# A four-layer graph kernel: two biases given by one-row products, two row weightings on VectorE

## The chip, the core and the metric

The kernel runs on one core of a Trainium2 chip. Five engines work side by side, each through its own queue in order: TensorE (PE), VectorE (DVE), ScalarE (ACT), GpSimd (POOL) and SyncE (SP, which only issues DMAs). They wait for each other by semaphores. The metric is the device time of one execution in microseconds (us), as the median of several.

## What is computed

50,000 nodes with 256 features each, 25,000 edges (12,500 pairs, both ways) and a loop at every node pass through four graph layers, each with a residual and a normalisation. Cut to what matters:

```python
x = layernorm(x + L0(x))          # two hypergraph convolutions, PReLU
# L1: attention over edges, 8 heads of 32
sent = x @ W_s + b_s;  recv = x @ W_r + b_r
logits = einsum(leaky_relu(sent[src] + recv[dst]), a_w) + a_b
w = softmax of logits over the edges of each dst
x = layernorm(x + segment_sum(w * sent[src], dst))
# L2: attention, 4 heads of 32, then a projection
x = layernorm(x + (segment_sum(alpha * h[src], dst) + bias) @ Wp + bp)
# L3: attention, 4 heads of 64, relu, rows divided by their norm
x = layernorm(x + L3(x))
```

The weights of one node sum to one, so `b_s` goes through the sum of L1 unchanged. In L2 the two biases come out as one row, called `bc`.

## The kernel before, in words

Nodes are split in two kinds. Those with edges are sorted into 50 groups of 512 rows (`ng` = 50, four chunks `k` of 128), and pass through seven stages, `p` = 0 to 6, group by group; `q = p * 50 + i` names a group in a stage. Stages 0 to 2 are the hops of L0. Stage 3 ends L0 and prepares L1 (its time in the profile is about 1820 to 2810 us). Stage 4 is L1's attention and the preparation of L2 (to 3890 us), stage 5 is L2's attention and projection (to 4610 us), stage 6 is L3 (to the end, 5534 us). A stage begins when the last has stored its tables. The nodes without edges need only dense products: the **dense pipeline**, 49 blocks of 512 rows (`dense_parts`), which may run at any time from stage 1 on.

The order on each engine isn't written by hand. `schedule` lists every step with its engine (T TensorE, S ScalarE, V VectorE, G GpSimd, Y SyncE), name and group, what it comes after, and its length from the table `TOOK`; the planner `Plan.run` lays the steps out, and each engine's queue follows that order. So a longer entry in `TOOK` also moves the dense blocks, which fill the gaps.

Steps that the change touches, by their names:

- Stage 3, per group: `x1b` (VectorE, L2113 and four row additions L2053 in `add_rows`) makes the rows of L1's input; `norm` (ScalarE, L1463) normalises them into `res`; `tp0`, `tp1` turn them (L1061) into `xl_t`. `tab0`, `tab1` multiply by `ws` (L1070) to give `sent`, and `r0`, `r1` multiply by `wr`, with `br` added in L2129 for `recv`. `ez` (L2138, L2141) forms the leaky sum in `z`, or in `sm` for some groups. `ew` on GpSimd (L2535) multiplies it by the attention weights `aw`. `es` on VectorE (L2145, L2147) sums to logits. `br` holds `b_r` plus `b_s`, since `tab` has no bias.
- `xb` on GpSimd (L2547), stages 3 and 4: after the rows have been turned, it adds the bias row to `res` (`bs_c` in stage 3 for L1, `bc` in stage 4 for L2), and `xst` (SyncE, L2736) stores the sum as the residual that the next stage loads into `xo`.
- Stage 4: `vals` (VectorE, L2286, L2287) weights the gathered rows; `mine` on GpSimd (L2541, L2542) weights the group's own rows by `pp`. `agg0` to `agg3` on TensorE (L1273) sum the chunks, and VectorE carries a row from one chunk to the next (L2161, L2163) and adds the own rows (L2315). `merge` divides (L2333) and adds the residual (L2053).
- Stage 5: `wp0`, `wp1` multiply by `wp` (L1283), and VectorE adds `xo` (L2343).
- Stage 4 has besides, on VectorE, the leaky sum of the edges' logits (L2188) and a running maximum (L2235), and on TensorE small products (L1261, L1262). The dense pipeline's lines are L1910 to L1969 and the statistics after them on VectorE, and L1061, L1070, L1083, L1107 and L1114 on TensorE.
- GpSimd also issues all gathers and scattered stores (L2460, L2456, L2551) and takes small powers (L2518, 128x4).

## Time and profile before

| | us |
|---|---|
| median of 3 runs | 5526.51 |
| lowest, highest | 5526.36, 5539.13 |
| the profiled execution, its own time | 5536.22 |
| its span | 5534.1 |
| TensorE clock granted, mean | 0.833 |
| device memory moved | 919.07 MB, 166 GB/s |

All durations below come from the one profiled execution, whose own time is 10 us above the median; 2 us of it lie outside the span. A busy time counts a moment once, however many instructions overlap in it, while a mean or median is of single instructions. An instruction that an engine has begun and that stands still counts as busy.

### The profile page before, as it was taken

The numbers are of one execution on the slowest core, as the hardware profiler recorded it, in microseconds if no ns is written. First come the engines' busy times: TensorE is split into PE (matmuls) and PEld (weight loads), VectorE is DVE, ScalarE is ACT, GpSimd is POOL, SyncE is SP. The second block draws the span as 40 slices with busy tenths as digits, with TensorE's granted clock in tenths as the row PEclk, the third lists the DMA queues.
The fourth block names the chain that finished last, engine by engine and source line by source line (L and its number), as shares of the span: only waits on it lengthen the run. The fifth ranks groups of instructions, "written<-read, shape, count | busy, mean of one in ns | idle before, by whom it ended". The sixth has DMA issues, their size and how long they took to land. (4 is left out here: it accounts for less than half of the span.)

```text
span 5534.1 us, 80216 instructions
## 1 busy us (share of the span) xinstructions
PE 4378.5 (79%) x19786; PEld 3284.9 (59%) x19786; DVE 3950.4 (71%) x10982; ACT 3033.9 (55%) x8955; POOL 3477.4 (63%) x2992
## 2 busy tenths in 40 slices
PE   0674349999999988888888898888899998767664
PEld 0541126666776767767666676666777786555442
DVE  8732114445776789888878777788888887888886
ACT  0233235555898666665654454455544556666655
POOL 2777777764777766666556556565644435777786
PEclk9855569999999999989998888888898999776555
DMA  1887644444666555555344444443455553444453
GB/s 41 274 288 267 189 131 149 153 161 140 222 217 205 189 179 176 191 174 180 143 141 156 143 158 160 147 157 125 121 181 182 195 185 124 133 136 125 147 156 99
DMA packets 360952, 919.07 MB, mean 166 GB/s; under 512 B 70931, under 2 KB 144781, under 8 KB 360496
## 3 DMA queue, kind: packets, MB, share of 16 engines
q1 hardware_dynamic: 250048, 639.69, 34.2%
q0 software_dynamic: 110448, 274.25, 16.5%
q8 instruction: 170, 2.79, 0.2%
q14 instruction: 286, 2.34, 0.1%
HBM read 578.85 MB, written 340.23 MB: 166 GB/s over the span
## 5 line engine op out<-in xcount | busy, mean ns | idle before, releaser
L2460 POOL DMA_INDIRECT got<-tab,end_i x600 | 700.7, 1168 | 481.7 <-PE psum L1273 319.6
L1158 PE MATMUL psum<-got,sf 128*128 128x256 f32 x1600 | 622.6, 477 | 353.4 <-ACT got L1425 279.4
L2460 POOL DMA_INDIRECT got<-hop,end_i x600 | 631.1, 1052 | 285.5 <-issue 166.7
L1158 PEld LDWEIGHTS psum<-got,sf 128*128 128x128 f32 x1600 | 327.2, 227 | 570.8 <-DMA got<-in_x,src_i 218.5
L1273 PE MATMUL psum<-got,sf 128*128 128x264 f32 (+2 forms) x1200 | 449.0, 463 | 266.6 <-DVE got L2164 166.8
L1425 ACT COPY got<-psum 1x256 f32<-1x256 f32 x796 | 282.3, 355 | 387.8 <-PE psum L1158 318.4
L1273 PEld LDWEIGHTS psum<-got,sf 128*128 128x128 f32 x1200 | 232.6, 231 | 391.2 <-DVE got L2164 222.6
L2090 DVE TENSOR_TENSOR res<-psum,own 128x512 f32<-128x512 f32 x300 | 206.4, 688 | 338.4 <-DMA own<-in_x,node_i 149.7
L1463 ACT ACTIVATE res<-res,l_mo 128x256 f32<-128x256 f32 x600 | 309.9, 588 | 185.2 <-DVE l_mo L2044 184.7
L1315 ACT ACTIVATE squares<-res,l_sv 128x256 f32<-128x256 f32 x600 | 296.9, 497 | 168.0 <-DVE l_sv L2056 110.4
L1429 ACT ACTIVATE res<-res,invc 128x256 f32<-128x256 f32 x600 | 270.8, 498 | 210.3 <-DVE res L2090 209.5
L1411 ACT CAST sf<-s 128x512 f32<-128x512 uint8 x350 | 214.4, 613 | 283.7 <-DVE s L2071 150.2
L2460 POOL DMA_INDIRECT x_in<-in_x,dn_i x196 | 219.1, 1118 | 145.4 <-PE psum L1061 67.6
L2518 POOL TENSOR_TENSOR l_mo<-l_mo,power 128x4 f32<-128x4 f32 x150 | 170.9, 1140 | 204.3 <-DVE l_mo L2121 202.3
L2551 POOL DMA_INDIRECT out<-res,out_i x200 | 235.1, 1175 | 98.8 <-issue 57.2
L1061 PE MATMUL psum<-ident,res 128*128 128x128 f32 x1600 | 257.2, 286 | 32.7 <-ACT res L1429 16.3
L2456 POOL DMA_INDIRECT out<-hd,dn_i x196 | 222.8, 1137 | 91.1 <-issue 53.6
L1303 ACT COPY xl_t<-psum 128x512 f32<-128x512 f32 x400 | 230.8, 580 | 82.0 <-PE psum L1061 79.4
L1061 PEld LDWEIGHTS psum<-ident,res 128*128 128x128 f32 x1600 | 202.2, 148 | 94.7 <-issue 38.2
L2460 POOL DMA_INDIRECT own<-in_x,node_i x200 | 208.9, 1045 | 72.9 <-issue 57.5
L2053 DVE SCALAR_TENSOR_TENSOR res<-res,xo 128x256 f32<-128x256 f32 x400 | 244.1, 664 | 3.4
L2460 POOL DMA_INDIRECT got<-in_x,src_i x200 | 204.2, 1021 | 60.9 <-issue 58.8
(497 smaller groups left out, 13253.6 us busy)
## 6 DMA issues: line engine op xcount, KB each, us to landing
own<-hop SPq DMA_DIRECT2D x150, 512.0 KB
x_t<-res SPq DMA_DIRECT2D x150, 512.0 KB, 2.7
xo<-x_t SPq DMA_DIRECT2D x150, 512.0 KB
hop<-res SPq DMA_DIRECT2D x100, 512.0 KB, 4.5
tab<-tab SPq DMA_DIRECT2D x50, 536.0 KB
own<-tab SPq DMA_DIRECT2D x50, 536.0 KB
r_t<-rec_b SPq DMA_DIRECT2D x50, 528.0 KB, 2.9
rec_b<-r_t SPq DMA_DIRECT2D x50, 528.0 KB, 3.9
```

What stands on the lines that cost most here:

```text
L1061: i = T.transpose(o[:, k * P:(k + 1) * P], src[:, k, c * P:(c + 1) * P], ident[:])
L1158: T.matmul(o, sf_of(q)[:, k * P:(k + 1) * P], got_of(q)[:, k * FEAT:(k + 1) * FEAT], start=(p < 3), stop=True).then_inc(at("l_agg"), 1)
L1273: T.matmul(bank(3 + k % 2)[:, 0:g.ext], sf_[:, k * P:(k + 1) * P], got_of(q)[:, k * g.width:k * g.width + g.ext], start=True, stop=True).t ...
L1303: S.copy(dst, filled_bank(eng, name, q)[:, 0:dst.shape[1]]).then_inc(at("s_out"), 1)
L1315: i = S.activation(squares[:, k, :], src[:, k, :], ACT.Square, bias=bias, scale=scale, accum_out=acc[:, k:k + 1])
L1425: S.copy(got_of(to)[0:1, c * FEAT:(c + 1) * FEAT], bank(3 + h // 2)[0:1, (h % 2) * FEAT:(h % 2 + 1) * FEAT]).then_inc(at("l_carry"), 1)
L1429: m = S.mul(res_of(q)[:, k, :], res_of(q)[:, k, :], invc[:, k, i:i + 1])
L1463: m = S.activation(res_of(q)[:, k, :], res_of(q)[:, k, :], ACT.Identity, bias=l_mo[:, par, 7, k:k + 1], scale=l_mo[:, par, 6, k:k + 1])
L2053: m = V.scalar_tensor_tensor(res_of(q)[:, k, :], res_of(q)[:, k, :], 0.0, xo_of(q)[:, k, :], ALU.add, ALU.add, accum_out=l_sv[:, par, 0, k ...
L2456: eng.indirect_dma_start(out=out, out_offset=bass.IndirectOffsetOnAxis(ap=dn_i[:, d * K + k:d * K + k + 1], axis=0), in_=hd[:, d % 3, k, : ...
L2460: eng.indirect_dma_start(out=dst, out_offset=None, in_=table, in_offset=bass.IndirectOffsetOnAxis(ap=idx, axis=0), bounds_check=rows_ - 1, ...
L2551: eng.indirect_dma_start(out=out, out_offset=bass.IndirectOffsetOnAxis(ap=out_i[:, k, i:i + 1], axis=0), in_=res_of(q)[:, k, :], in_offset ...
```

## The change

Four things change. `xb` is gone from GpSimd: `res` is stored as it is. In its place the bias enters the product: `tab0` and `tab1` of stage 3 (`biased_product`) and `wp0` and `wp1` of stage 5 begin each of their two sums with a product of a row of ones and the bias row, over one row of contraction. `br` loses `bs_c`, since `tab` now carries it. The multiplication by `aw` goes from GpSimd into `es` on VectorE, and stage 4's `mine` goes to VectorE. Additions into `res` wait for `l_sh` besides. `TOOK` and the steps' lengths follow.

```diff
-    "Tscan": 0.44, "Tspr": {4: 1.75, 5: 0.88, 6: 0.88}, "Tt3t": 0.44, "Ttab0": {3: 1.73, 4: 0.93, 5: 0.91}, "Ttab1": {3: 1.73, 4: 0.93, 5: 0.91},
+    "Tscan": 0.44, "Tspr": {4: 1.75, 5: 0.88, 6: 0.88}, "Tt3t": 0.44, "Ttab0": {3: 2.59, 4: 0.93, 5: 0.91}, "Ttab1": {3: 2.59, 4: 0.93, 5: 0.91},
-    "Ves": 1.56, "Vez": 2.77, "Vfrs": 0.22, "Vh": 0.66, "Vhd": 0.79, "Vlead": {4: 0.92, 5: 0.2, 6: 0.34}, "Vlogit": 0.66,
-    "Vmax": {4: 0.55, 5: 0.15, 6: 0.15}, "Vmerge": {4: 4.16, 5: 1.15, 6: 1.68}, "Vmine": {5: 0.62, 6: 1.15}, "Vmo": 0.83, "Vnode": 0.15, "Voh": 0.42,
+    "Ves": 2.76, "Vez": 2.77, "Vfrs": 0.22, "Vh": 0.66, "Vhd": 0.79, "Vlead": {4: 0.92, 5: 0.2, 6: 0.34}, "Vlogit": 0.66,
+    "Vmax": {4: 0.55, 5: 0.15, 6: 0.15}, "Vmerge": {4: 4.16, 5: 1.15, 6: 1.68}, "Vmine": {4: 1.4, 5: 0.62, 6: 1.15}, "Vmo": 0.83, "Vnode": 0.15, "Voh": 0.42,
...
-                    put(("V", "x1b", q), 2.95, here("Sx1a") + ([("S", "sqv", q - 2)] if i >= 2 else []))
+                    put(("V", "x1b", q), 2.95, here("Sx1a") + ([("S", "sqv", q - 2), ("V", "sh", q - 2)] if i >= 2 else []))
-                if p < 5:
-                    put(("G", "xb", q), 2.5, here("Ttp0", "Ttp1"))
-                put(("Y", "xst", q), 0.35, here("Snorm" if p == 5 else "Gxb"), landing=3.0)
+                put(("Y", "xst", q), 0.35, here("Snorm"), landing=3.0)
-                put(("G", "ew", q), 2.8, here("Vez"))
-                put(("V", "es", q), 1.6, here("Gew"))
+                put(("V", "es", q), 2.8, here("Vez"))
-                me = "Gmine" if p == HOPS else "Vmine"
-                put((me[0], "mine", q), 3.1 if p == HOPS else 0.75, here("Sexp", "Yown"))
+                put(("V", "mine", q), 1.4 if p == HOPS else 0.75, here("Sexp", "Yown"))
-                    put(("V", f"agg{k}", q), 0.78 if p != 5 else 0.5, here(f"Tagg{k}", me))
+                    put(("V", f"agg{k}", q), 0.78 if p != 5 else 0.5, here(f"Tagg{k}", "Vmine"))
-                put(("V", "merge", q), {4: 3.2, 5: 1.0, 6: 1.7}[p], here("Vagg3") + ([("S", "sqv", q - 2)] if p == 4 else []) + free_ + (here("Yxo") if p == 4 else []) + early("V", "merge", 1))
+                put(("V", "merge", q), {4: 3.2, 5: 1.0, 6: 1.7}[p], here("Vagg3") + ([("S", "sqv", q - 2), ("V", "sh", q - 2)] if p == 4 else []) + free_ + (here("Yxo") if p == 4 else []) + early("V", "merge", 1))
-                put(("V", "u", q), 1.8, here("Grn", "Yxo") + [("S", "sqv", q - 2)] * (i >= 2))
+                put(("V", "u", q), 1.8, here("Grn", "Yxo") + [("S", "sqv", q - 2), ("V", "sh", q - 2)] * (i >= 2))
...
+        def biased_product(eng, name, q, h, rows_t, w, bias):
+
+            o = free_bank(eng, name, q)
+            for k in (2 * h, 2 * h + 1):
+                here = o[:, (k % 2) * FEAT:(k % 2 + 1) * FEAT]
+                T.matmul(here, ones[:], bias[0:1, :], start=True, stop=False)
+                for c in range(2):
+                    if k == 2 * h:
+                        eng.wait_ge(at("s_out"), ev_no[f"tp{c}", q])
+                    i = T.matmul(here, rows_t[:, c, k * P:(k + 1) * P], w[:, c, :], start=False, stop=(c == 1))
+            i.then_inc(at("t_fill"), 1)
...
+                rows_t = xl_t[:, large["xl"].slot(q)]
+                if p == 3:
+                    biased_product(eng, name, q, h, rows_t, ws, bs_c)
+                    return
                 for c in range(2):
                     eng.wait_ge(at("s_out"), ev_no[f"tp{c}", q])
-                rows_t = xl_t[:, large["xl"].slot(q)]
-                if p == 3:
-                    half_product(eng, name, q, h, rows_t, ws)
-                elif p == 4:
+                if p == 4:
...
-                eng.wait_ge(at("s_out"), ev_no["tz", q])
                 o = free_bank(eng, name, q)
                 for k in (2 * h, 2 * h + 1):
                     here = o[:, (k % 2) * FEAT:(k % 2 + 1) * FEAT]
-                    m = T.matmul(here, zt[:, k * P:(k + 1) * P], wp[:], start=True, stop=True)
+                    T.matmul(here, ones[:], bc[0:1, :], start=True, stop=False)
+                    if k == 2 * h:
+                        eng.wait_ge(at("s_out"), ev_no["tz", q])
+                    m = T.matmul(here, zt[:, k * P:(k + 1) * P], wp[:], start=False, stop=True)
...
+                V.memset(ones[:], 1.0)
...
+                done(V.tensor_tensor(br[:], br[:], bs_c[:], ALU.subtract))
...
             if ln_of(q) >= 2:
                 eng.wait_ge(at("d_sq"), sq_done["sqv", q - 2][1])
                 eng.wait_ge(at("l_nm"), ln_of(q) - 1)
+                eng.wait_ge(at("l_sh"), ln_of(q) - 1)
...
             elif name == "es":
                 rows_ = by_chunk(rec_of(q), recv_w)
+                zh = z_of(q).rearrange("p (m c) -> p m c", c=cols1)
+                eng.wait_ge(at("l_ez"), i + 1)
+                V.tensor_tensor(zh, zh, over(aw[:], K * heads1), ALU.mult).then_inc(at("l_ew"), 1)
                 eng.wait_ge(at("l_ew"), i + 1)
...
+            elif name == "mine" and p == HOPS:
+                eng.wait_ge(at("g_p"), j + 1)
+                eng.wait_ge(*own_landed(q))
+                c4, weight = split_heads(own_f, g), by(pp[:, par, 1, 0:hk])
+                V.tensor_tensor(c4, c4, weight.unsqueeze(3).to_broadcast([P, K, g.heads, g.cols]), ALU.mult)
+                V.tensor_copy(own_f[:, :, g.flat:g.ext], weight).then_inc(at("g_w"), 1)
...
-            elif name == "ew":
-                eng.wait_ge(at("l_ez"), i + 1)
-                zh = z_of(q).rearrange("p (m c) -> p m c", c=cols1)
-                G.tensor_tensor(zh, zh, over(aw[:], K * heads1), ALU.mult).then_inc(at("l_ew"), 1)
-            elif name == "mine":
-                eng.wait_ge(at("g_p"), i + 1)
-                eng.wait_ge(*own_landed(q))
-                own_f = by_chunk(own_of(q), g1.width)
-                c4, weight = split_heads(own_f, g1), pp[:, par, 1, 0:K * heads1].rearrange("p (k h) -> p k h", k=K)
-                G.tensor_tensor(c4, c4, weight.unsqueeze(3).to_broadcast([P, K, heads1, cols1]), ALU.mult)
-                G.tensor_copy(own_f[:, :, g1.flat:g1.ext], weight).then_inc(at("g_w"), 1)
-            elif name == "xb":
-
-                eng.wait_ge(at("l_ln"), ln_of(q) + 1)
-                eng.wait_ge(at("t_fill"), max(fill_no["tp0", q], fill_no["tp1", q]) + 1)
-                G.tensor_tensor(res_of(q), res_of(q), over((bs_c if p == 3 else bc)[:], K), ALU.add).then_inc(at("l_xb"), 1)
...
-                    eng.wait_ge(at("l_xb"), q - stop_a + 1)
+                    eng.wait_ge(at("l_ln"), ln_of(q) + 1)
```

The planner then gives other orders. GpSimd, from the first groups of stage 3 on, before:

```order
L2547 TENSOR_TENSOR res<-res,bs_c 128x1024
L2518 TENSOR_TENSOR l_mo<-l_mo,power 128x4
L2460 DMA got<-hop,end_i 128x256 x4
L2460 DMA x_in<-in_x,dn_i 128x256 x4
L2535 TENSOR_TENSOR z<-z,aw 128x1024
L2547 TENSOR_TENSOR res<-res,bs_c 128x1024
L2460 DMA got<-hop,end_i 128x256 x4
L2535 TENSOR_TENSOR z<-z,aw 128x1024
L2518 TENSOR_TENSOR l_mo<-l_mo,power 128x4
```

and now:

```order
L2485 DMA got<-hop,end_i 128x256 x4
L2485 DMA x_in<-in_x,dn_i 128x256 x4
L2543 TENSOR_TENSOR l_mo<-l_mo,power 128x4
L2485 DMA got<-hop,end_i 128x256 x4
L2481 DMA out<-hd,dn_i 50000x256 x4
L2543 TENSOR_TENSOR l_mo<-l_mo,power 128x4
```

The 128x1024 operations on rows are gone; gathers, stores and the 128x4 powers remain.

VectorE, where a group of stage 3 ends (`z` the leaky sum, `rec_b` the receiver rows), before:

```order
L2138 TENSOR_TENSOR z<-tab,rec_b 128x1024
L2141 SCALAR_TENSOR_TENSOR z<-z 128x1024
L1931 BN_STATS d_bn<-psum 128x6 x2
L2129 TENSOR_TENSOR rec_b<-psum,br 128x2x256
L2145 TENSOR_REDUCE rec_b<-z 128x4x8
L2147 SCALAR_TENSOR_TENSOR rec_b<-rec_b,ab,hostc 128x4x8
L2129 TENSOR_TENSOR rec_b<-psum,br 128x2x256
L2113 SCALAR_TENSOR_TENSOR res<-z,oma,res 128x1024
```

and now:

```order
L2153 TENSOR_TENSOR z<-tab,rec_b 128x1024
L2156 SCALAR_TENSOR_TENSOR z<-z 128x1024
L2123 SCALAR_TENSOR_TENSOR res<-psum,invc,xo 128x256 x2
L2161 TENSOR_TENSOR z<-z,aw 128x1024
L2163 TENSOR_REDUCE rec_b<-z 128x4x8
L2165 SCALAR_TENSOR_TENSOR rec_b<-rec_b,ab,hostc 128x4x8
L1945 BN_STATS d_bn<-psum 128x6 x2
L2144 TENSOR_TENSOR rec_b<-psum,br 128x2x256
L2128 SCALAR_TENSOR_TENSOR res<-z,oma,res 128x1024
```

The product with `aw` (L2161) stands between the leaky sum and the reduction, with one other group's step ahead of it.

TensorE in the middle of stage 5 (`t3w` the next layer's weights, `got` the gathered rows), before:

```order
L1238 MATMUL psum<-ms,sm 128x8 x4
L1076 MATMUL psum<-t3w,xl_t 128x268 x2
L1283 MATMUL psum<-wp,lgt 128x256 x2
L1076 MATMUL psum<-t3w,xl_t 128x268 x2
L1283 MATMUL psum<-wp,lgt 128x256 x2
L1076 MATMUL psum<-t3w,xl_t 128x268 x2
L1273 MATMUL psum<-got,sf 128x132
L1076 MATMUL psum<-t3w,xl_t 128x268 x2
```

and now:

```order
L1283 MATMUL psum<-got,sf 128x132
L1085 MATMUL psum<-t3w,xl_t 128x268 x2
L1292 MATMUL psum<-bc,ones 128x256
L1295 MATMUL psum<-wp,lgt 128x256
L1292 MATMUL psum<-bc,ones 128x256
L1295 MATMUL psum<-wp,lgt 128x256
L1283 MATMUL psum<-got,sf 128x132
L1260 MATMUL psum<-ident,fmax 128x4 x4
```

Each product with `wp` has a product with `bc` in front.

The dense blocks move too. Counted in the two orders on TensorE, the first product of 20, 33, 41 and 44 of the 49 blocks stood ahead of the first product of stages 3, 4, 5 and 6; now it is 20, 30, 37 and 40. Stage 3 thus holds 10 instead of 13 blocks, stage 4 holds 7 instead of 8, stage 5 holds 3 as before, and stage 6 holds 9 instead of 5. On GpSimd the stores of dense rows (`out<-hd`) now stand among the very last entries:

```order
L2560 DMA out<-res,out_i 50000x256 x4
L2481 DMA out<-hd,dn_i 50000x256 x4
L2551 TENSOR_TENSOR l_ss<-l_ss,power 128x4 x2
L2543 TENSOR_TENSOR l_mo<-l_mo,power 128x4 x2
L2560 DMA out<-res,out_i 50000x256 x4
L2551 TENSOR_TENSOR l_ss<-l_ss,power 128x4
L2560 DMA out<-res,out_i 50000x256 x4
L2481 DMA out<-hd,dn_i 50000x256 x4
L2543 TENSOR_TENSOR l_mo<-l_mo,power 128x4
L2481 DMA out<-hd,dn_i 50000x256 x4
L2560 DMA out<-res,out_i 50000x256 x4
```

Before, the last of them stood 65 rows ahead of the end.

## Rows read from the trace of the kernel before

**Rows 1.** busy time, share of the span, instructions of each engine: part 1 of the page
```profile
PE 4378.5 (79%) x19786; PEld 3284.9 (59%) x19786; DVE 3950.4 (71%) x10982; ACT 3033.9 (55%) x8955; POOL 3477.4 (63%) x2992
```

**Rows 2.** by stretch, us: PE, PEld, DVE, ACT, POOL busy (instructions), clock, DMA share, GB/s
```profile
1840.00:2800.00 960.00, 840.57 (x3706) 675.97 (x3706) 816.49 (x1631) 596.67 (x1661) 608.74 (x421) 0.93 0.51 173
2820.00:3890.00 1070.00, 925.61 (x4950) 701.75 (x4950) 832.89 (x2377) 546.49 (x1528) 613.07 (x445) 0.85 0.45 148
3900.00:4610.00 710.00, 658.96 (x3738) 549.97 (x3737) 589.33 (x2153) 369.72 (x1106) 305.65 (x285) 0.93 0.53 170
4625.00:5300.00 675.00, 466.97 (x1862) 340.13 (x1861) 580.43 (x1937) 441.97 (x1588) 504.68 (x422) 0.68 0.44 138
5300.00:5500.00 200.00, 119.82 (x402) 82.43 (x402) 160.38 (x512) 110.63 (x407) 149.08 (x124) 0.50 0.44 136
```

**Rows 3.** the same view, the last stretch of stage 5
```profile
4480.00:4620.00 140.00, 138.22 (x774) 113.57 (x773) 112.44 (x385) 80.89 (x255) 39.72 (x36) 1.00 0.41 141
```

**Rows 4.** timeline, 1977 to 1985 us: start, duration, instruction
```profile
1978.48 0.42 DVE L2053 SCALAR_TENSOR_TENSOR res<-res,xo 128x256 f32<-128x256 f32 x1
1978.83 5.47 DVE L2053 SCALAR_TENSOR_TENSOR res<-res,xo 128x256 f32<-128x256 f32 x1
1979.34 2.38 POOL L2535 TENSOR_TENSOR z<-z,aw 128x1024 f32<-128x1024 f32 x1
1981.65 2.36 POOL L2547 TENSOR_TENSOR res<-res,bs_c 128x1024 f32<-128x1024 f32 x1
```

**Rows 5.** groups of GpSimd tensor instructions: busy us, mean ns | idle before
```profile
L2547 POOL TENSOR_TENSOR res<-res,bs_c 128x1024 f32<-128x1024 f32 x50 | 124.4, 2489 | 41.6 <-PE psum L1061 41.4
L2547 POOL TENSOR_TENSOR res<-res,bc 128x1024 f32<-128x1024 f32 x50 | 121.6, 2433 | 85.3 <-PE psum L1061 84.8
L2541 POOL TENSOR_TENSOR own<-own,pp 128x1024 f32<-128x1024 f32 x50 | 115.1, 2302 | 104.7 <-ACT pp L1499 104.4
L2535 POOL TENSOR_TENSOR z<-z,aw 128x1024 f32<-128x1024 f32 x34 | 87.1, 2561 | 38.6 <-DVE z L2141 35.3 <-PE psum L1070 2.7
```

**Rows 6.** groups of VectorE instructions, same columns
```profile
L2053 DVE SCALAR_TENSOR_TENSOR res<-res,xo 128x256 f32<-128x256 f32 x400 | 244.1, 664 | 3.4
L2287 DVE COPY got<-pp 128x32 f32<-128x32 f32 x50 | 43.5, 869 | 0.0
L2235 DVE TENSOR_TENSOR_SCAN fmax<-opn,fmax,lgt 8x512 f32<-8x512 f32 x49 | 70.3, 1434 | 2.3 <-DVE lgt L2233 0.3
```

**Rows 7.** single lines of VectorE: duration ns min/median/max, starts
```profile
L2053 DVE SCALAR_TENSOR_TENSOR res<-res,xo x400: 412/419/5474, 1828.7 to 3866.8; 128x256 f32<-128x256 f32 x134
L2287 DVE COPY got<-pp x50: 161/180/2347, 2852.2 to 3847.9; 128x32 f32<-128x32 f32 x50
L2235 DVE TENSOR_TENSOR_SCAN fmax<-opn,fmax,lgt x49: 1271/1272/3097, 2854.1 to 3835.2; 8x512 f32<-8x512 f32 x49
L2188 DVE SCALAR_TENSOR_TENSOR z<-z x50: 1202/1215/7392, 2835.0 to 3819.3; 128x1024 f32<-128x1024 f32 x50
```

**Rows 8.** groups of TensorE products; each product leaves two records
```profile
L1283 PE MATMUL psum<-wp,lgt 128*128 128x256 f32 x400 | 108.9, 397 | 1.9 <-DVE d_bn L1931 1.9
L1262 PE MATMUL psum<-ident,lgt 8*128 8x16 f32 x400 | 86.3, 289 | 0.0
L1261 PE MATMUL psum<-rec_b,sm 128*128 128x16 f32 x400 | 82.8, 283 | 10.7 <-DVE rec_b L2254 7.9 <-DVE y1t L1916 2.4 <-DVE hd L1960 0.2
```

**Rows 9.** first and last group of the dense pipeline, VectorE then TensorE
```profile
L1910 DVE SCALAR_TENSOR_TENSOR h_t<-h_t,oma,psum 128x512 f32<-128x512 f32 x98 | 72.5, 740 | 37.2 <-ACT h_t L1329 36.5 <-issue 0.3
L1969 DVE SCALAR_TENSOR_TENSOR hd<-hd,d_ra,t3d 128x256 f32<-128x256 f32 x196 | 87.4, 504 | 0.0
L1083 PE MATMUL psum<-xt,w 128*128 128x512 f32 x392 | 192.5, 615 | 1.6 <-ACT xt L1303 0.6 <-ACT squares L1352 0.6 <-DVE y1t L1916 0.3
L1114 PE MATMUL psum<-ident,y1t 128*128 128x128 f32 x392 | 61.8, 282 | 0.4 <-DVE h_t L1910 0.2
```

**Rows 10.** waits of VectorE, whole span: us, times, longest
```profile
DVE rec_b L2145 <- POOL sm L2535: 9.1, 6, 2.4
```

More of the change, by code:

```diff
@@ L624, in build_program @@
         cbs = sb("cbs", [P, 1])
+        ones = sb("ones", [1, P])
         w3 = sb("w3", [P, 2, FEAT])
@@ L2358, in vector_gat @@
                     eng.wait_ge(at("d_sq"), sq_done["sqv", q - 2][1])
+                    eng.wait_ge(at("l_sh"), ln_of(q) - 1)
                 V.scalar_tensor_tensor(l_sv[:, par, 1, :], l_sv[:, par, 0, :], -1.0 / (16 * FEAT), l_ss[:, par, 2, :], ALU.mult, ALU.mult)
```

2 rows, old and new, of the table TOOK are left out of this document.

## The prediction

> **What bounds the kernel now.** I read the page's busy times first, then the same engines by stage, then the durations of single lines, then the timeline at the longest ones. Over the span TensorE is busy 79%, VectorE 71%, GpSimd 63% [rows 1]: no engine is full, so the answer lies in the stages. In stage 3 TensorE is busy 841 of 960 us (0.88) and VectorE 816 (0.85); in stage 4, 926 (0.87) and 833 (0.78) of 1070; in stage 5, 659 (0.93) and 589 (0.83) of 710; in stage 6 up to 5300 us VectorE leads with 580 of 675 (0.86), TensorE's clock falling to 0.50 [rows 2]. GpSimd is never the fullest, and VectorE waited for its product at L2535 and its weighted rows only a few times [rows 10]. Going by that alone, taking work from GpSimd would buy nothing.
>
> The durations say otherwise. Line L2053 adds 128x256 rows in 419 ns at the median, 5474 at the most, 664 on average; L2287, a small copy, has 180, 2347 and 869; L2188 has 1215 and 7392 [rows 6, 7]. The timeline shows why: such an addition starts at 1978.83 and lasts 5.47 us, while GpSimd runs the two 128x1024 operations L2535 and L2547 back to back until 1984.01; the same addition 0.35 us earlier took 0.42 [rows 4]. VectorE stands still, counted as busy, while GpSimd works on rows. The Trainium skill (SBUF — State Buffer, Who interferes with whom) says that a VectorE instruction with two SBUF inputs and a GpSimd one that reads SBUF exclude each other, the later one waiting for all of the other; by that rule, the trace agrees for L2053 and L2188.
>
> The price: count times (mean minus median). L2053: 400 x 0.245 = 98 us. L2287: 50 x 0.689 = 34. Twelve lines of this kind, with L2053 as the first and L2235 (49 x 0.162 = 8) as the last, sum to 265 us [rows 6, 7]. Lines that run in stage 3 alone carry 43 of it and those of stage 4 alone 86; the 136 of the shared lines I split 100 to 36 by the lines' busy time in the two stages. So stage 3 has 143 us of standing still and stage 4 122.
>
> **The change part by part.**
>
> *GpSimd's work goes.* The four groups of [rows 5] sum to 448 us, and two small ones go too. GpSimd had time to spare, so its own time counts at nothing; what hides it is VectorE's and TensorE's work, and it stays hidden since GpSimd only gets emptier. What counts is VectorE's standing still: bounds 0 (the others hide it) and -265 x 1.5 (others queue behind the engine that stands). I take about one for one before the next limit.
>
> *VectorE gets two operations.* The product with `aw`: 50 x 1.22 = 61 us, priced by a 128x1024 operation of two SBUF inputs undisturbed, 1215 ns. Own rows: 50 x (1.22 + 0.18) = 70 us, the copy at 180 ns [rows 7]. Behind them in VectorE's queue stand the next groups' additions and carry steps.
>
> *TensorE gets 400 one-row products* of 256 columns, 200 in stage 3 and 200 in stage 5. No such product is in the trace; the nearest row of the same width is `wp`'s: 400 records for 200 products, 108.9 us, so 0.545 us each [rows 8], 109 us per stage. From below: a product over 8 rows is recorded at 289 ns, one over 128 rows at 283 [rows 8], so few rows save nothing; zero is the floor if all of it fell into TensorE's gaps. I take 109. The Trainium skill (TensorE: Matmul & The Clock Gate, Why this matters for your kernels) says a product over 32 rows takes as long as one over 128; these rows agree for 8, and it is the rule that speaks against this change.
>
> *The planner moves the dense pipeline.* With longer entries it puts 10 instead of 13 of the 49 blocks of rows without edges into stage 3, 7 instead of 8 into stage 4, 3 as before into stage 5, and 9 instead of 5 into stage 6. A block costs TensorE 1176/49 = 24.0 us (8 groups, the first and the last in [rows 9]) and VectorE 706/49 = 14.4 us (9 groups, same place) plus some twenty short statistics instructions, an estimate of 17 us in all.
>
> *Stage 3.* VectorE: 816 - 143 + 61 - 3 x 17 = 683. TensorE: 841 + 109 - 3 x 24 = 878. TensorE now sets the stage. At the old share of 0.88 the stage would take about 1000 us; in the last part of stage 5 TensorE was busy 138 of 140 us at clock 1.00 [rows 3], which would give 878/0.987 = 890. VectorE at about 0.75 leaves it few waits, and a fuller TensorE was granted a higher clock in this trace (1.00 against 0.93) [rows 2, 3]. I take 900: **-60**.
>
> *Stage 4.* VectorE: 833 - 122 + 70 - 17 = 764; TensorE 926 - 24 = 902, nothing added. VectorE's own balance is -69, and TensorE, which waits for its carried rows here, gains part of what it lost at clock 0.85 [rows 2]. Bounds -30 and -160. **-100**.
>
> *Stage 5.* TensorE 659 + 109 = 768 of what were 710 us. At the old share 827; at the share of [rows 3] and with half of what its clock would give (1.00 against 0.93) about 750 (768 x 0.965 / 0.987). VectorE changes nothing here. **+70**, between +35 and +117.
>
> *Stage 6.* Four more blocks, 68 us more on VectorE, the fullest engine. After 5300 us, where before has no dense work, VectorE is busy 160 of 200 [rows 2], so some of it goes into gaps. **+60**, between +20 and +100.
>
> *Joins of stages.* The last group of stages 3 and 4 leads to the patch and the next stage over these GpSimd steps: 2.4 for `ew`, 2.5 and 2.4 for `xb`, 2.3 for `mine` [rows 5], less 2.6 on VectorE: **-7**.
>
> Sum: -60 - 100 + 70 + 60 - 7 = -37. From the profiled execution's own 5536 us (span 5534) this gives 5499; the median of the runs is 10 below the profiled one, so 5489, said as 5490.
>
> New waits: the additions wait for the shift `sh` of two groups earlier, which stands ahead of them on VectorE itself, so nothing is queued behind it. The store `xst` goes one GpSimd step earlier, and nobody waits for it but the ring.
>
> **The rivals.**
>
> *A, the forecast:* the above, 5490; its own range is 5430 to 5550. Chance 0.50.
>
> *B, standing still cost more than its length.* ScalarE and GpSimd wait for VectorE's sums, so 5 us on VectorE delay three queues. Stage 3 then ends at TensorE's best, -85; stage 4 gives -122 x 1.5 + 70 - 17 = -130; stage 5 +50, stage 6 +40; with the joins about -132, so 5395. For it: GpSimd ran the two operations back to back only because both were due [rows 4]. Against it: TensorE is nearly as full as VectorE. Chance 0.18.
>
> *C, TensorE becomes the bound, on the slower side.* If TensorE's gaps are not VectorE's doing, it keeps share and clock: stage 3 878/0.875 = 1003 (+43), stage 5 +117, stage 4 902/0.865 = 1043 (-27), stage 6 +60, joins -7: +186, or 5712. It decides at a share of about 0.92 in stages 3 and 5: below it the change loses. A third to half of that way is 5580 to 5620. For it: the added products are full price. Against it: [rows 3] shows a share of 0.99. Chance 0.19.
>
> *D, it cancels:* stage 4's gain is only VectorE's balance, -69, and stage 3 stays at -40 while stages 5 and 6 take +110: -6, or 5520. Chance 0.13.
>
> **How the numbers follow.** Within 0.3% (about what a measurement of this kernel can tell from no change) means 5510 to 5543. Faster: 0.40 of A, all of B, 0.03 of D: 0.61. Same: 0.06 of A, 0.08 of D: 0.14. Slower: 0.04 of A, 0.02 of D, all of C: 0.25. The range reaches down to B and below it to 5380, and up into C, to 5600; outside lie a deeper B and the far half of C.
>
> **What the profile after would show.** L2053's line (L2068 now) at a mean near its median 0.42 us; VectorE's busy time down by 265 - 131 = 134 us to about 3816; GpSimd's down by at least the 448 of the four groups, to 3030 or less; TensorE's up by at most 218. Stage 3 about 900 us with TensorE at 0.95, stage 4 about 970, stage 5 about 780, stage 6 about 60 longer with dense stores up to its last groups. Wrong would be: means still far above medians (something else blocks VectorE), a one-row product well under 0.5 us, or TensorE's share in stages 3 and 5 unchanged.

## The result: 2.1% slower, and the profile after

The kernel after takes 5642.5 us at the median of 4 runs (5638.9 to 5665.7), before 5527.0 in the same comparison: ratio 1.0213, 95% interval 1.0182 to 1.0243. The forecast was 5490. The profiled execution has a span of 5642.6 us at a mean granted clock of 0.853.

Busy times, share of the span and instructions, part 1 of the page of after (against [rows 1]):

```profile
PE 4622.3 (82%) x20586; PEld 3323.0 (59%) x20586; DVE 3776.6 (67%) x11134; ACT 3046.6 (54%) x8955; POOL 3009.3 (53%) x2742
```

VectorE lost 174 us and GpSimd 468, as meant. TensorE gained 244, more than the 218 that the forecast gave as the most.

The view by stretch of after: stages 3, 4, 5, the larger part of 6 and 200 us of its end (against [rows 2]); columns are the stretch, its length, PE, PEld, DVE, ACT, POOL busy (instructions), clock, DMA share, GB/s:

```profile
1825.00:2755.00 930.00, 914.49 (x3999) 673.28 (x3997) 692.49 (x1600) 587.78 (x1582) 386.93 (x325) 0.99 0.55 185
2765.00:3815.00 1050.00, 919.15 (x4891) 681.86 (x4890) 752.67 (x2475) 544.93 (x1527) 357.22 (x291) 0.86 0.45 148
3830.00:4655.00 825.00, 806.88 (x4044) 589.04 (x4043) 579.01 (x2088) 354.93 (x1055) 293.90 (x269) 0.91 0.44 142
4675.00:5400.00 725.00, 495.10 (x2016) 353.83 (x2014) 609.00 (x1981) 470.27 (x1679) 548.43 (x452) 0.72 0.43 134
5400.00:5600.00 200.00, 137.94 (x555) 100.19 (x554) 177.67 (x605) 133.00 (x498) 128.24 (x110) 0.67 0.36 114
```

TensorE is busy 98% of stages 3 and 5 and sets them. In stage 4 neither it (88%) nor VectorE (72%) is full.

To compare many kernels I give stage lengths from each stage's first marked instruction to the next one's (stage 3: TensorE's first turning of `own`; 4: its first product with `awb`; 5 and 6: VectorE's first `sl`), so joins are included; stage 6 ends with GpSimd's last instruction. Before, they are 1022, 1074, 712 and 904 us; after, 943, 1065, 838 and 976. The differences, -80, -9, +127 and +72, with -3 before stage 3, sum to +107. The two profiled spans differ by 108.5; the last 1.3 us lie behind GpSimd's last instruction. Each set of stage lengths comes from one execution. Executions of one kernel can differ by 10 to 27 us in all, so a few us between two kernels in one stage mean nothing.

VectorE's standing still is gone. The addition into `res` in after (before: 664 ns on average, [rows 6]):

```profile
L2068 DVE SCALAR_TENSOR_TENSOR res<-res,xo 128x256 f32<-128x256 f32 x400 | 146.3, 421 | 3.4
```

Over all VectorE instructions at least 150 ns above their median, that excess fell from 324 us to 18. (The forecast's 265 us came from twelve lines; by this count stage 3 held 169 us before and stage 4 144.)

What came in its place is on TensorE. The bias products (L1292, L1066), the products that follow them (L1295, L1070) and the weight loads (PEld) of both, in after; columns: group | busy us, mean ns of one | idle before and what ended it:

```profile
L1292 PE MATMUL psum<-bc,ones 1*128 1x256 f32 x400 | 148.2, 452 | 0.0
L1295 PE MATMUL psum<-wp,lgt 128*128 128x256 f32 x400 | 151.4, 463 | 0.0
L1066 PE MATMUL psum<-bs_c,ones 1*128 1x256 f32 x400 | 139.5, 428 | 2.9 <-DVE t3d L1958 2.1 <-DVE hd L1974 0.8
L1070 PE MATMUL psum<-ws,xl_t 128*128 128x256 f32 x800 | 227.8, 407 | 0.0
L1292 PEld LDWEIGHTS psum<-bc,ones 1*128 1x128 f32 x400 | 62.3, 194 | 58.0 <-issue 53.3 <-DVE tab L2147 1.0 <-DVE fm L2289 0.2
L1295 PEld LDWEIGHTS psum<-wp,lgt 128*128 128x128 f32 x400 | 63.6, 200 | 72.1 <-issue 67.2 <-ACT xl_t L1315 5.0
L1066 PEld LDWEIGHTS psum<-bs_c,ones 1*128 1x128 f32 x400 | 58.8, 184 | 71.8 <-issue 60.3 <-DVE rec_b L2144 4.6 <-DVE t3d L1958 2.5
L1070 PEld LDWEIGHTS psum<-ws,xl_t 128*128 128x128 f32 x800 | 136.3, 190 | 77.2 <-issue 66.3 <-ACT tab L1494 0.3
```

Two records are one product. The one-row product took 148.2 / 200 = 0.74 us, not 0.545, and the `wp` product behind it went from 0.545 [rows 8] to 0.76. The loads stood idle "<-issue" some 60 us a group. The timeline of TensorE in stage 5 shows where:

```profile
4203.48 0.29 PEld L1292 LDWEIGHTS psum<-bc,ones 1*128 1x128 f32 x2 [0.35 <-issue]
4203.48 0.69 PE L1292 MATMUL psum<-bc,ones 1*128 1x256 f32 x2
4204.10 0.30 PEld L1295 LDWEIGHTS psum<-wp,lgt 128*128 128x128 f32 x2 [0.33 <-issue]
4204.10 0.70 PE L1295 MATMUL psum<-wp,lgt 128*128 128x256 f32 x2
4204.73 0.29 PEld L1292 LDWEIGHTS psum<-bc,ones 1*128 1x128 f32 x2 [0.33 <-issue]
4204.73 0.69 PE L1292 MATMUL psum<-bc,ones 1*128 1x256 f32 x2
```

Each load begins only with its own product: 0.62 us from product to product. The Trainium skill (TensorEngine Tiling (Array Packing), Key Properties) says that changing the array's tiling mode, unlike changing the tile, drains the engine. If a product over 1 row and one over 128 stand in two modes, each change between them costs an overlap. The prediction didn't weigh that rule; the next runs test it.

The trace of before holds such changes too. Its product L1250 over 4 rows follows one over 128 rows (`t3w`) 17 times, and each time the load stood idle for at least 0.35 us, as here in stage 5:

```profile
4123.88 0.75 PEld L1076 LDWEIGHTS psum<-t3w,xl_t 128*128 128x128 f32 x4
4124.99 0.32 PEld L1250 LDWEIGHTS psum<-ident,fmax 4*128 4x128 f32 x4 [0.35 <-issue]
```

The two groups that the prediction compared, L1261 over 128 rows and L1262 over 8 [rows 8], stand next to each other, and a product starts every 0.32 us there:

```profile
3069.34 0.40 PE L1261 MATMUL psum<-rec_b,sm 128*128 128x16 f32 x2
3069.66 0.39 PE L1262 MATMUL psum<-ident,lgt 8*128 8x16 f32 x2
3069.98 0.40 PE L1261 MATMUL psum<-rec_b,sm 128*128 128x16 f32 x2
```

Small products over 128 rows among their like (L1264, 4 columns) start every 0.22 us. So 289 and 283 ns are alike in two groups that both stand in an alternation with wider spacing.

### The profile page after: what moved, and what is told of

Its sections match the earlier page's. It is cut to its first block and busy times, and to the rows that moved or that the text cites. A ratio compares the mean times of both kernels' runs of the same rounds, so it can differ in the third digit from the quotient of the medians.

```text
span 5642.6 us, 81508 instructions
## 1 busy us (share of the span) xinstructions
PE 4622.3 (82%) x20586; PEld 3323.0 (59%) x20586; DVE 3776.6 (67%) x11134; ACT 3046.6 (54%) x8955; POOL 3009.3 (53%) x2742
## 5 line engine op out<-in xcount | busy, mean ns | idle before, releaser
L2485 POOL DMA_INDIRECT got<-tab,end_i x600 | 714.4, 1191 | 772.5 <-PE psum L1283 608.4
L1283 PE MATMUL psum<-got,sf 128*128 128x264 f32 (+2 forms) x1200 | 423.3, 440 | 280.4 <-DVE got L2182 176.7
L1167 PEld LDWEIGHTS psum<-got,sf 128*128 128x128 f32 x1600 | 323.1, 224 | 556.1 <-DMA got<-in_x,src_i 217.4
L1283 PEld LDWEIGHTS psum<-got,sf 128*128 128x128 f32 x1200 | 223.5, 221 | 415.2 <-DVE got L2182 225.3
L1058 PE MATMUL psum<-ident,res 128*128 128x128 f32 x1600 | 254.6, 284 | 23.6 <-ACT res L1441 16.3
L1058 PEld LDWEIGHTS psum<-ident,res 128*128 128x128 f32 x1600 | 202.4, 147 | 81.6 <-issue 31.4
L1085 PE MATMUL psum<-t3w,xl_t 128*128 128x268 f32 x800 | 240.0, 426 | 0.2
```

The costliest lines, as they stand in the source:

```text
L1058: i = T.transpose(o[:, k * P:(k + 1) * P], src[:, k, c * P:(c + 1) * P], ident[:])
L1085: m = T.matmul(o, rows_t[:, c, k * P:(k + 1) * P], w[:, c, :], start=(c == 0), stop=(c == 1))
L1167: T.matmul(o, sf_of(q)[:, k * P:(k + 1) * P], got_of(q)[:, k * FEAT:(k + 1) * FEAT], start=(p < 3), stop=True).then_inc(at("l_agg"), 1)
L1283: T.matmul(bank(3 + k % 2)[:, 0:g.ext], sf_[:, k * P:(k + 1) * P], got_of(q)[:, k * g.width:k * g.width + g.ext], start=True, stop=True).t ...
L2485: eng.indirect_dma_start(out=dst, out_offset=None, in_=table, in_offset=bass.IndirectOffsetOnAxis(ap=idx, axis=0), bounds_check=rows_ - 1, ...
```

## Experiments

All ratios are to the kernel before, run in the same comparison, with 95% intervals. "After" is 1.0213.

### What the bias products cost

**Without them.** The two lines are left out and `start` goes to the next product, so the biases are missing from the output; the order is that of after.

```diff
-                T.matmul(here, ones[:], bias[0:1, :], start=True, stop=False)
-                    T.matmul(here, ones[:], bc[0:1, :], start=True, stop=False)
```

> The changed kernel in the same order without the bias products; the two biases are left out. It gives their whole cost. Theory T: stage 5 back to 700 to 720 us (-120 to -140), stage 3 -60 to -90, stages 4 and 6 as in the changed kernel, total 5420 to 5460. If the loss came from the placing of the dense blocks instead, the total would be above 5560.

5369.5 us, 0.9714 (0.9696 to 0.9733). So the 400 one-row products cost 273 us of time, and all the rest of the change is worth -157. Stages 3 and 5 take 822 and 679 us; by that the products cost 121 us in stage 3 and 159 in stage 5. Stages 4 and 6 take 1073 and 968. `wp`'s product has its old length again:

```profile
L1293 PE MATMUL psum<-wp,lgt 128*128 128x256 f32 x400 | 110.3, 400 | 1.8 <-ACT lgt L1313 1.7
```

**Over all 128 rows**, in the same order and with the same number of products:

```diff
-        ones = sb("ones", [1, P])
+        ones = sb("ones", [P, P])
-                V.memset(ones[:], 1.0)
+                V.memset(ones[:], 1.0 / P)
-                T.matmul(here, ones[:], bias[0:1, :], start=True, stop=False)
+                T.matmul(here, ones[:], bias[:, :], start=True, stop=False)
```

(and `bc[:, :]` for `bc[0:1, :]`)

> The changed kernel in the same order, with each bias product over 128 rows (weights 1/128, the bias row in all partitions) instead of one row; same count and width of products. Theory S (it is the switch between a one-row and a 128-row product that costs: 0.74 us for the one-row product and 0.21 us more for its neighbour, against 0.545 for a product among equals): product and neighbour fall to about 0.5 each, stage 5 is 60 to 90 us shorter, stage 3 30 to 60, total 5500 to 5560. Theory N (a third product costs that much whatever its rows): total 5640 as the changed kernel.

**5447.7 us, 0.9848 (0.9825 to 0.9870): 195 us less than after, the shortest time here of a kernel that computes everything** (the ratio of the last run below is lower, but not clear of it). Stage 3 takes 865, stage 5 711; stages 4 and 6 are as after (1070, 973). Groups, then the timeline in stage 5, then stages 3 and 5 by stretch:

```profile
L1292 PE MATMUL psum<-bc,ones 128*128 128x256 f32 x400 | 122.5, 388 | 0.1
L1295 PE MATMUL psum<-wp,lgt 128*128 128x256 f32 x400 | 120.8, 384 | 0.0
L1070 PE MATMUL psum<-ws,xl_t 128*128 128x256 f32 x800 | 207.1, 382 | 0.0
L1292 PEld LDWEIGHTS psum<-bc,ones 128*128 128x128 f32 x400 | 72.1, 193 | 8.9 <-ACT lgt L1315 0.3 <-DVE tab L2147 0.2
L1295 PEld LDWEIGHTS psum<-wp,lgt 128*128 128x128 f32 x400 | 77.2, 193 | 10.8
```

```profile
4040.18 0.60 PE L1292 MATMUL psum<-bc,ones 128*128 128x256 f32 x2
4040.40 0.41 PEld L1295 LDWEIGHTS psum<-wp,lgt 128*128 128x128 f32 x2
4040.62 0.59 PE L1295 MATMUL psum<-wp,lgt 128*128 128x256 f32 x2
4040.83 0.41 PEld L1292 LDWEIGHTS psum<-bc,ones 128*128 128x128 f32 x2
4041.05 0.59 PE L1292 MATMUL psum<-bc,ones 128*128 128x256 f32 x2
```

```profile
1830.00:2660.00 830.00, 816.21 (x3899) 689.95 (x3899) 679.10 (x1562) 566.02 (x1521) 371.43 (x308) 0.99 0.59 200
3770.00:4450.00 680.00, 660.46 (x3965) 569.56 (x3963) 559.46 (x2043) 340.76 (x1008) 279.10 (x256) 0.98 0.52 170
```

Each load now begins while the product before it runs, and products start every 0.43 us instead of 0.62 (the granted clock is 1.00 around both timelines). For the 400 products of `bc` and `wp` that is 76 of the 127 us between the two stages 5; in the rest the clock has a part (0.98 here, 0.91 in after). Full-row products cost 78 us in all (5447.7 less 5369.5), a one-row product 3.5 times as much.

**Over 32 and 64 rows.** For 32:

```diff
-        ones = sb("ones", [1, P])
+        ones = sb("ones", [32, P])
-                V.memset(ones[:], 1.0)
+                V.memset(ones[:], 1.0 / 32)
-                T.matmul(here, ones[:], bias[0:1, :], start=True, stop=False)
+                T.matmul(here, ones[:], bias[0:32, :], start=True, stop=False)
```

> The changed kernel in the same order, with bias products over 32 rows (weights 1/32) instead of one. Theory S32 (any product over a part of the 128 rows next to one over all of them costs the extra time): as the changed kernel, total about 5640, 0.70 us or more for each bias product. Theory S1 (the cost comes from a single row alone): as with full rows, total about 5450, 0.6 us each.

> The same over 64 rows. Theory S32: total about 5640. Theory S1: about 5450. A third outcome: between the two, if the cost grows with the rows left out.

5641.9 us, 1.0204 (1.0180 to 1.0228) and 5614.4, 1.0154 (1.0132 to 1.0176). The bias product of stage 5, over 32 and then over 64 rows:

```profile
L1292 PE MATMUL psum<-bc,ones 32*128 32x256 f32 x400 | 148.1, 451 | 0.0
```

```profile
L1292 PE MATMUL psum<-bc,ones 64*128 64x256 f32 x400 | 145.1, 444 | 0.1
```

So it isn't the single row: any count of 1, 32 or 64 next to 128 pays, 128 next to 128 doesn't. That is what the drain at a change of mode, cited above from the Trainium skill (TensorEngine Tiling (Array Packing), Key Properties), would do, and the trace agrees with it; no run here shows the drain itself. The kernel with 64 rows is 28 us faster than after, and the intervals don't overlap. Its products start 0.62 us apart too where the clock is 1.00, but in stage 5 (805 us) it was granted 0.95, and after 0.91.

**The biases alone**, `ew` and `mine` left on GpSimd as before, one-row products:

```diff
-                put(("V", "es", q), 2.8, here("Vez"))
+                put(("G", "ew", q), 2.8, here("Vez"))
+                put(("V", "es", q), 1.6, here("Gew"))
-                put(("V", "mine", q), 1.4 if p == HOPS else 0.75, here("Sexp", "Yown"))
+                me = "Gmine" if p == HOPS else "Vmine"
+                put((me[0], "mine", q), 3.1 if p == HOPS else 0.75, here("Sexp", "Yown"))
```

> The change's bias part alone: one-row products in stages 3 and 5, no bias additions on GpSimd; the product with aw and the own rows' weighting stay on GpSimd. Theory T: stage 5 as long as in the changed kernel (838 us), stage 3 960 to 1000, total 5630 to 5680. Theory V: under 5600, since stage 3 and 4 keep part of the relief and stage 5's loss is made up.

5635.2 us, 1.0198 (1.0174 to 1.0222). Stages 971, 1062, 843, 921. The loss is this part's.

### What VectorE's standing still is worth

**The weightings alone**, with `br` and the lengths of the products as before:

```diff
-                put(("Y", "xst", q), 0.35, here("Snorm"), landing=3.0)
+                if p < 5:
+                    put(("G", "xb", q), 2.5, here("Ttp0", "Ttp1"))
+                put(("Y", "xst", q), 0.35, here("Snorm" if p == 5 else "Gxb"), landing=3.0)
-                T.matmul(here, ones[:], bias[0:1, :], start=True, stop=False)
-                    T.matmul(here, ones[:], bc[0:1, :], start=True, stop=False)
```

> The change's VectorE part alone: the product with aw and stage 4's weighting of own rows on VectorE; the bias additions stay on GpSimd (xb), no one-row products, the planner's lengths of tab and wp as before. Theory T (TensorE bounds stages 3 to 5, and the added products are the whole loss): no TensorE work is added, so stage 5 is back at 711 us and the total is 5500 to 5535. Theory V (VectorE's standing still bounded stages 3 and 4, and the loss has other causes, such as where the dense blocks went): half of the standing still goes (the share of L2535 and L2541), and the total is 5400 to 5460.

5496.5 us, 0.9940 (0.9923 to 0.9958). Stages 942, 1083, 700, 946: stage 3 gives 80 us and stage 5 12, stages 4 and 6 lose 9 and 42. With `xb` left, 169 of the 324 us of excess remain.

**The standing still alone.** The kernel before with its order, but GpSimd's three operations on 128x1024 elements cut to 128x4, so that rows stay unweighted and biases are missing:

```diff
-                G.tensor_tensor(zh, zh, over(aw[:], K * heads1), ALU.mult).then_inc(at("l_ew"), 1)
+                G.tensor_tensor(zh[:, 0:4, 0], zh[:, 0:4, 0], aw[:, 0:1].to_broadcast([P, 4]), ALU.mult).then_inc(at("l_ew"), 1)
```

> The kernel before, in its own order, with GpSimd's four row operations cut from 128x1024 to 128x4 (biases, attention weights and own rows' weights are then missing on all but a few elements). It takes VectorE's standing still away and changes nothing else. The forecast's step: stage 3 about -85 to -140, stage 4 -100 to -120, total 5290 to 5340. Theory T4: stage 4 is bound by TensorE and stays within 25 us of 1074; stage 3, where VectorE was 0.85 busy, gains 60 to 140; total 5390 to 5460.

5337.4 us, 0.9653 (0.9632 to 0.9674). Excess 12 us; stages 888, 1006, 708, 899. No work was taken from TensorE or VectorE, but GpSimd lost its own 431 us. The page's first part:

```profile
PE 4288.8 (81%) x19786; PEld 3235.3 (61%) x19786; DVE 3647.4 (69%) x10982; ACT 3034.7 (57%) x8955; POOL 3046.1 (57%) x2992
```

So the standing still was worth 193 us, together with GpSimd's own time, which this run can't part from it. VectorE had waited for the results of these operations for 16 us in all. Stage 3 gives 134 us of the 143 that the forecast put there, stage 4 68 of 122.

### Other ways to give the bias

**Stage 4's `xb` kept on GpSimd, no bias product in stage 5**, the rest as with full rows:

```diff
+                if p == 4:
+                    put(("G", "xb", q), 2.5, here("Ttp0", "Ttp1"))
-                    T.matmul(here, ones[:], bc[:, :], start=True, stop=False)
```

> The kernel with full-row bias products in stage 3, but stage 4 keeps the bias addition on GpSimd (xb, 50 times 2.4 us) and stage 5 has no bias product. If standing still of VectorE in stage 4 is hidden, stage 4 stays at 1070 and stage 5 goes from 711 to about 680: total 5410 to 5430. If it isn't hidden, stage 4 grows by 40 to 75 and the total is 5450 or more. The planner puts one more dense block into stage 6, about 18 us more there.

5452.1 us, 0.9864 (0.9842 to 0.9886), no different from full rows. Stage 4 takes 1093 and stage 6 955, with VectorE at 822 us in stage 4 instead of 761. Stage 5 takes 708, not the 680 expected, though it holds no bias product. The kernel without any bias products takes 679 there, with the same products. What differs in stage 5 is the plan: this kernel is planned with 0.87 for `wp`, that one with 1.73.

**Besides, stage 3's bias added by VectorE** as it takes `tab` out of PSUM in ScalarE's place, with no bias product anywhere:

```diff
+                if p == 3:
+                    V.tensor_tensor(tab_of(q)[:, h * ROWS:(h + 1) * ROWS].rearrange("p (k f) -> p k f", k=2),
+                                    filled_bank(eng, name, q).rearrange("p (k f) -> p k f", k=2), over(bs_c[:], 2), ALU.add).then_inc(at("v_out"), 1)
```

> As the kernel with the addition kept in stage 4 alone, but without any bias product: in stage 3 the bias is added by VectorE as it takes the product from PSUM (100 operations of 0.69 us), in place of ScalarE's copy. TensorE, busy 0.98 of stage 3, is relieved of 71 us, VectorE gets 69: stage 3 falls from 865 to about 840, total 5385 to 5410. If VectorE then bounds stage 3 there is no gain over its neighbour.

5480.6 us, 0.9911 (0.9888 to 0.9933). Stage 3 is 924, 59 more than with full-row products, with VectorE at 777 us. But this kernel is also planned with before's 1.73 for `tab0` and `tab1`. The full-row kernel planned with that and other lengths of before takes 923 in stage 3 too (below), and there VectorE has no bias to add. So this run doesn't show that the bias is dearer on VectorE than on TensorE.

### Why stage 4 gained nothing

**Less of TensorE's or of VectorE's work.** From the full-row kernel, half of the attention product in stage 4 is left out; or VectorE's weighting of the gathered rows is:

```diff
-                for c in range(2):
-                    m = T.matmul(o[0:g.heads, :], awb[:, c, :], z[:, par, c * ROWS:(c + 1) * ROWS], start=(c == 0), stop=(c == 1))
+                m = T.matmul(o[0:g.heads, :], awb[:, 0, :], z[:, par, 0:ROWS], start=True, stop=True)
```

> The kernel with full-row bias products, in the same order, leaving out one of the two products (8 columns of weights, 512 columns streamed) of stage 4's logits; half of the features are missing from them. It takes 50 products of about 1.2 us from TensorE in stage 4. Theory T4 (stage 4 is bound by TensorE, busy 935 of 1070 us whatever VectorE does): stage 4 falls from 1070 to 1000 to 1025, total from 5448 to 5385 to 5405. Theory K (stage 4 is bound by the chain of carried rows between TensorE and VectorE): stage 4 moves by less than 15 us.

```diff
-                V.tensor_tensor(c4, c4, weight.unsqueeze(3).to_broadcast([P, K, g.heads, g.cols]), ALU.mult)
```

> The kernel with full-row bias products, in the same order, leaving out VectorE's weighting of the gathered rows in stage 4 (50 operations of 1.22 us; their weights are missing). Theory T4: stage 4 stays within 15 us of 1070. Theory V4 (VectorE's work sets stage 4): it falls by 50 to 60 us.

0.9818 (0.9798 to 0.9839) and 0.9864 (0.9843 to 0.9884). 30 us less of TensorE give stage 4 28 us (1042); 55 us less of VectorE give nothing (1075 against 1070). VectorE's balance, on which the forecast of -100 rested, doesn't count there.

**Dense blocks placed as after, in the kernel before:**

```diff
+        held = [("T", "agg0", 4 * 50)] * (d >= 30) + [("T", "agg0", 5 * 50)] * (d >= 37) + [("T", "agg0", 6 * 50)] * (d >= 40)
-        add(("G", "xin", d), 4.8, [ ("T", "x0", d - 2), ("T", "x1", d - 2)], landing=2.5)
+        add(("G", "xin", d), 4.8, [ ("T", "x0", d - 2), ("T", "x1", d - 2)] + held, landing=2.5)
```

> The kernel before with the dense blocks held to the changed kernel's places (10, 7, 3 and 9 blocks in stages 3 to 6 in place of 13, 8, 3, 5), nothing else changed. By the forecast's terms: stage 3 -50 to -70, stage 4 -15 to -24, stage 6 +60 to +75, total within 25 us of 5527. If the placing were a large part of the changed kernel's loss, the total would be 5570 or more.

1.0014 (1.0002 to 1.0025): stages 1013, 1058, 719, 927. Placing the blocks otherwise costs next to nothing. Stage 6 grows by 23 us and stage 3 shrinks by 9, where 60 to 75 and 50 to 70 were expected.

**Four kernels that differ in plan.** First the last two edits together (blocks placed, GpSimd's operations small). Then the biases alone with full rows and GpSimd's `ew` and `mine` small. Then the full-row kernel with VectorE's `mine` small. In all three rows are left unweighted, and in the first biases are missing too. The edit of the third:

```diff
-                V.tensor_tensor(c4, c4, weight.unsqueeze(3).to_broadcast([P, K, g.heads, g.cols]), ALU.mult)
+                V.tensor_tensor(c4[:, :, 0, 0], c4[:, :, 0, 0], weight[:, :, 0], ALU.mult)
```

> Before, with GpSimd's operations on rows cut to 128x4 (as the run that gave 5337) and the dense blocks held to 10, 7, 3 and 9 a stage as in the plan after. If only the places of the dense blocks make stage 4 long without standing still: stage 4 near 1055, total near 5400. If the placing costs what it cost with the operations in full: stage 4 about 990 (1006 less 16), stage 6 about 920, total about 5350.

> The kernel that only moves the biases (ew and mine stay on GpSimd), with products over 128 rows, and GpSimd's two operations on rows cut to 128x4, so that VectorE neither stands still nor has the two operations. Its plan differs from that of before only by the biases. If mine on VectorE was what cost stage 4 its gain: stage 4 near 1006, total near 5340 plus 78 for the products, less 10 for the joins, about 5400. If it is the order: stage 4 at 1050 to 1070 and 5440 to 5460.

> The kernel with full-row bias products (5448 us), with VectorE's weighting of the own rows in stage 4 cut from 128x1024 to 128x4 elements (the copy stays); order and everything else as there. About 55 us of VectorE work less. If that work in VectorE's queue, ahead of the carried rows, is why stage 4 did not gain: stage 4 falls from 1070 to about 1010 and the total to about 5390. If the order of the plan or TensorE sets the stage: 1060 to 1075, total 5440 to 5453.

5314.5 us, 0.9605 (0.9589 to 0.9621); 5380.0, 0.9730 (0.9711 to 0.9748); 5438.4, 0.9840 (0.9824 to 0.9857). Stage 4 by stretch, in that order, and last the full-row kernel:

```profile
2690.00:3650.00 960.00, 876.03 (x4845) 669.35 (x4844) 685.55 (x2339) 533.75 (x1478) 405.05 (x440) 0.88 0.49 161
```

```profile
2715.00:3710.00 995.00, 894.92 (x4812) 679.99 (x4813) 675.39 (x2315) 528.04 (x1478) 381.31 (x376) 0.86 0.47 154
```

```profile
2690.00:3725.00 1035.00, 918.59 (x4851) 684.31 (x4851) 691.16 (x2439) 537.31 (x1511) 329.96 (x285) 0.85 0.45 149
```

```profile
2695.00:3740.00 1045.00, 909.73 (x4840) 676.98 (x4841) 741.30 (x2435) 538.10 (x1510) 354.06 (x285) 0.85 0.45 148
```

All four have 7 dense blocks, give or take half a one, and the same products in stage 4 (some 4,840 records), and the first three nearly the same VectorE work. Yet stage 4 takes 968, 1019, 1059 and 1070 us. TensorE is idle for 84, 100, 116 and 135 us of these stretches. Its clock falls from 0.88 to 0.85, and the same products keep it busy for longer (876, then 895, 919 and 910 us). The own rows' 128x1024 work on VectorE costs 11 us (1059 to 1070). The 91 between 968 and 1059 come with the plan: 51 when the biases leave GpSimd, 40 when `ew` and `mine` change queue. The placing isn't it: the first of the four has it too. That it is the plan is argued by exclusion.

**The full-row kernel planned with before's lengths** for the products and `es`, and 0.2 us for `mine`. The work is the same; only the order differs. The changed entries of `TOOK`, cut and put together:

```diff
-    "Ttab0": {3: 2.59, ...}, "Ttab1": {3: 2.59, ...}, "Twp": 1.73, "Ves": 2.76, "Vmine": {4: 1.4, ...}
+    "Ttab0": {3: 1.73, ...}, "Ttab1": {3: 1.73, ...}, "Twp": 0.87, "Ves": 1.56, "Vmine": {4: 0.2, ...}
```

> The kernel with full-row bias products, planned with the lengths that before had for the products with ws and wp and for es, and 0.2 us for mine, so that the order comes near that of before; the work is the same. If the order costs stage 4 its gain: stage 4 at 1000 to 1030, total 5390 to 5420, which would be the fastest kernel that computes everything. If not: within 10 us of 5448.

5512.0 us, 0.9975 (0.9964 to 0.9986), **64 us worse** than with honest lengths: stages 923, 1052, 768, 938. Stage 4 got 18 us better, stages 3 and 5 58 and 57 worse, though no instruction was added. My hope that the old lengths bring back the old order's 1006 fell. What it shows is how much the order alone is worth. The dense blocks are part of it: by their first products, stages 3 to 6 hold 10, 6, 4 and 9 here and 9, 7, 3 and 10 in the full-row kernel. At 24 us of TensorE each (the prediction's price), one block more accounts for less than half of what stages 3 and 5 lost. Stage 5 of this kernel:

```profile
3800.00:4545.00 745.00, 705.37 (x4044) 597.62 (x4043) 574.89 (x2083) 353.20 (x1046) 296.10 (x272) 0.96 0.49 158
```

**`mine` back on GpSimd in the full-row kernel:**

```diff
-                put(("V", "mine", q), 1.4 if p == HOPS else 0.75, here("Sexp", "Yown"))
+                me = "Gmine" if p == HOPS else "Vmine"
+                put((me[0], "mine", q), 3.1 if p == HOPS else 0.75, here("Sexp", "Yown"))
```

> The kernel with full-row bias products (5448 us), with the weighting of the own rows in stage 4 back on GpSimd, where before has it; all else as there. The plan puts 10, 7, 3 and 9 dense blocks into stages 3 to 6, as there. With the own rows' work cut small on GpSimd stage 4 was 1019, cut small on VectorE 1059, in full on VectorE 1070. If the order that the step takes in VectorE's queue is what costs: stage 4 at 1030 to 1045 and the total 5410 to 5425. If GpSimd's operation makes VectorE stand still for as much as the move would save: stage 4 at 1060 to 1070, total 5440 to 5450.

5959 us, 0.9808 (0.9760 to 0.9857). In this comparison before itself took 6085 us. The chip has the same number as the one of the full-row kernel's run, where before took 5533, so nothing on record makes it another chip; the cause of the longer times is open. Of the extra time of this kernel's profiled execution 395 us lie ahead of stage 3 (2214 us against 1819, with the same work); stage 4 takes 1079. The interval holds the full-row kernel's 0.9848. Which of the two is better stays open.

## Why the prediction was wrong, step by step

- **The engine that waits, not the one that works: right.** VectorE's standing still was there, it went (excess 324 to 18 us; L2068 at 421 ns where 0.42 us was forecast), and with GpSimd's own time it is worth 193 us. VectorE's busy time came to 3777 (forecast 3816), GpSimd's to 3009 (3030 or less). The Trainium skill's rule (SBUF — State Buffer, Who interferes with whom) held in every run: the additions are long only while GpSimd has operations on rows (all 37 long ones of before overlap one; the kernels without such operations have none above 0.49 us).
- **The one-row product, the step that failed first.** I priced it at 0.545 us, from `wp`'s row, and took 109 us a stage as the upper end. It is 0.74 us, and its neighbour pays 0.21 more. In time the 400 cost 273 us, against 218 even at full price: 121 in stage 3 and 159 in stage 5. Stage 5 came to +127 for a forecast of +70, beyond its bound of +117. The rows of 8-row products [rows 8] showed a length and I read it as a price; both groups stood in an alternation and both paid. What a change of rows does to the next load stood in none of the rows that I quoted, though the trace of before had it (L1076 then L1250), so the upper bound was none.
- **The rule against the change was the wrong one.** I cited the Trainium skill (TensorE: Matmul & The Clock Gate, Why this matters for your kernels): few rows take as long as 128. In this alternation they take longer: 452 ns a record over 1 row, 451 over 32, 444 over 64, 388 over 128. What the Trainium skill (TensorEngine Tiling (Array Packing), Key Properties) says of the drain at a change of mode fits all four counts.
- **Stage 3: right in sign, -80 for -60**, by two errors that partly cancel; that it came this near is luck. The products cost 121 us (943 against 822 without them) for 109 forecast. The rest of the change gave 200, where the forecast's 900 less its 110 for the products makes 170.
- **Stage 4, the second step that failed: -9 for -100.** The -100 was VectorE's balance with a bonus. Removing VectorE work there gives 0 for 55 us. Removing the standing still gives 68 in the old plan, and the new plan takes it away again: TensorE is idle longer and, at a lower clock, busy longer. I had moved only the dense blocks in my sum, which cost 1.0014 in all, and counted the rest of the new order at nothing.
- **Stage 6: the number right, +72 for +60, its reason not.** The term was four more dense blocks at 17 us. With those four moved there in the kernel before, stage 6 grew by 23 us only (927 against 904). What makes up the other 49 stays open.
- **Rivals.** The time lies towards C, but its reason is wrong: TensorE's share didn't stay at 0.88, it rose to 0.98 in stages 3 and 5. The forecast's share was about right and its product was too cheap. Stage 4 went worse than D has it.

By size: of the 144 us between the sum (-37) and the stage lengths (+107), stage 4 holds 91, stage 5 57, stage 6 12 and the joins 7, which the stage lengths include and no run parts off; stage 3 gives 20 back, and 3 lie ahead of it.

**Open:** which of the moved steps leaves TensorE idle in stage 4. VectorE's wait for the turned rows before the division (new: L2357 on L1058, 30 us in the full-row kernel) isn't in the kernel with the weightings alone, whose stage 4 is just as long. Stage 5 without bias products is 33 us shorter than before (679 against 712) with the same products. It is the plan as far as these runs show: planned with before's length for `wp` it takes 708. What in the plan does it is open too.
